# Weight preparation moved to one DMA queue, layer norm fused with the first projection, and the query mean and Wo load moved later

## What is computed

```python
xn = layernorm(x)
q, k, v = (split_heads(xn @ W + b) for W, b in ((Wq,bq),(Wk,bk),(Wv,bv)))
qf, kf, vf = rfft(q), rfft(k), rfft(v)            # over the 2048 positions, 1025 frequencies
idx  = top_k(mean(abs(qf)), 64)                    # per head
attn = softmax(sum(qf.real * kf.real) / 8) at idx
out_freq = mean of qf over the frequencies, everywhere
out_freq[idx] = attn * vf.real[idx]
attn_out = irfft(out_freq) @ Wo + bo
ffn_out  = (silu(xn @ wg) * (xn @ wu)) @ wd        # weights given as int32, scaled by 1/127
result   = x + attn_out + ffn_out
```

## Time and profile before

| | |
|---|---|
| time, median of 2 runs | 6702.76 us (6506.15 and 6899.37) |
| profiled execution | 6235.25 us |
| its span on the slowest core | 6233.7 us (8 cores: 6192.0 to 6233.7) |
| mean granted TensorE clock | 0.868 to 0.870 of full on all cores |
| busy, share of span | TensorE 75%, VectorE 21%, ScalarE 13%, GpSimd 4% |
| moved by DMA | 437.69 MB, 70 GB/s |

### The profile page before, as it was taken

How to read it: one execution, slowest core, us unless ns; L and a number is a source line. 1 busy time by engine, 2 the same in 40 slices (tenths; PEclk the granted TensorE clock), 3 DMA queues, 4 the chain that set the end, 5 groups by cost and what they waited for, 6 DMA issues and landing times.

```text
span 6233.7 us, 52442 instructions; the slowest of 8 cores (6192.0 to 6233.7 us)
## 1 busy us (share of the span) xinstructions
PE 4665.9 (75%) x20720; PEld 1969.4 (32%) x20720; DVE 1306.0 (21%) x1735; ACT 810.5 (13%) x940; POOL 249.8 (4%) x364
## 2 busy tenths in 40 slices
PE   2484627998919884899855884799991888589985
PEld 1131212443403332344322331244440333224442
DVE  3030121011132222111113322101113222211111
ACT  2010101111021111111003111111102111111100
POOL 0101000000100000000000000000010000000001
PEclk9796768999959897999976996899995998789998
DMA  3433332112232112111231311211223212211122
GB/s 104 116 83 113 105 98 76 46 39 65 96 114 48 41 51 78 49 48 38 94 107 58 75 48 47 75 49 39 68 91 117 44 41 58 65 57 50 38 89 93
DMA packets 509272, 437.69 MB, mean 70 GB/s; under 512 B 408524, under 2 KB 408652, under 8 KB 509032
## 3 DMA queue, kind: packets, MB, share of 16 engines
q1 hardware_dynamic: 465384, 279.12, 16.4%
q0 software_dynamic: 33280, 117.46, 6.0%
q10 hardware_dynamic: 10368, 37.75, 2.2%
HBM read 365.07 MB, written 69.21 MB: 70 GB/s over the span
## 4 chain that ended last, share of the span: by engine, by line
PE 62%; DMA 25%; DVE 7%; issue 4%; ACT 2%; DVEq 0%; POOL 0%; ACTq 0%; SPq 0%; POOLq 0%
PE pw L506 15%; PE pw L842 11%; PE pw L851 11%; PE pw L465 10%; PE pw L748 4%; PE pw L795 4%; DMA spE<-attn_scr 3%; DMA spB<-x 2%; DMA spA<-x 2%; DMA spE<-Wo 2%; DMA out<-spC 2%; PE pw L473 2%; PE pw L550 1%; DMA out<-spD 1%; ACT r L409 1%
## 5 line engine op out<-in xcount | busy, mean ns | idle before, releaser
L506 PE MATMUL pw<-r,strm 128*128 128x512 bf16 x4096 | 910.4, 386 | 399.0 <-DMA strm<-dft_cos 399.0
L465 PE MATMUL pw<-strm,r 128*128 128x512 bf16 x3072 | 761.6, 401 | 263.3 <-ACT r L477 101.4
L842 PE MATMUL pw<-r,strm 128*128 128x512 bf16 x3072 | 694.4, 379 | 0.0
L851 PE MATMUL pw<-r,strm 128*128 128x512 bf16 x3072 | 694.4, 379 | 0.0
L506 PEld LDWEIGHTS pw<-r,strm 128*128 128x128 bf16 x4096 | 405.7, 99 | 902.1 <-issue 435.7
L883 PE MATMUL pw<-r 128*128 128x512 bf16 x2048 | 470.0, 389 | 99.6 <-DMA r<-wdT_s 62.6
L861 DVE TENSOR_TENSOR r<-strm,pw 128x1024 bf16<-128x1024 bf16 x192 | 234.6, 1222 | 1382.0 <-PE pw L851 1382.0
L465 PEld LDWEIGHTS pw<-strm,r 128*128 128x128 bf16 x3072 | 291.0, 101 | 720.6 <-issue 434.1
L431 PE MATMUL pw<-identb_t,r 128*128 128x128 bf16 x512 | 64.7, 305 | 549.8 <-DVE r L425 493.3
L851 PEld LDWEIGHTS pw<-r,strm 128*128 128x128 bf16 x3072 | 300.6, 98 | 362.4
L842 PEld LDWEIGHTS pw<-r,strm 128*128 128x128 bf16 x3072 | 300.2, 98 | 363.2 <-issue 1.7
(11 more groups left out here) (142 smaller groups left out, 2631.8 us busy)
## 6 DMA issues: line engine op xcount, KB each, us to landing
strm<-dft_cos SPq DMA_DIRECT2D x96, 512.0 KB
r<-x SPq DMA_DIRECT2D x64, 512.0 KB
strm<-wgT_s SPq DMA_DIRECT2D x96, 256.0 KB
strm<-wuT_s SPq DMA_DIRECT2D x96, 256.0 KB
strm<-dft_sinn POOLq DMA_DIRECT2D x32, 512.0 KB, 5.6
spE<-Wo SPq DMA_DIRECT2D x32, 512.0 KB
r<-crt SPq DMA_DIRECT2D x8, 2048.0 KB
r<-cit SPq DMA_DIRECT2D x8, 2048.0 KB
```

Source lines behind the costliest of these rows:

```text
L465: e.matmul(pw[pwi][:, eta * 512:(eta + 1) * 512], xnT[:, dc, tau * 128:(tau + 1) * 128], wv[:, dc, eta * 512:(eta + 1) * 512], start=(dc = ...
L506: e.matmul(pw[pwi][:, eta * 512:(eta + 1) * 512], slotv[:, tau, :], sig[:, tau, eta * 512:(eta + 1) * 512], start=(tau == 0), stop=(tau == ...
L842: e.matmul(pw[pg][:, tq * 512:(tq + 1) * 512], wgv[:, dc, :], xnT[:, dc, th * 1024 + tq * 512:th * 1024 + (tq + 1) * 512], start=(dc == 0) ...
L851: e.matmul(pw[pu][:, tq * 512:(tq + 1) * 512], wuv[:, dc, :], xnT[:, dc, th * 1024 + tq * 512:th * 1024 + (tq + 1) * 512], start=(dc == 0) ...
```

## The change

- The keys sd and gc go. Each prep_chunk loads on SyncE's queue (q) and casts on VectorE (even) or ScalarE (odd). The prep_some calls are four of 18 chunks, around the second and third projection, in place of six of 12.
- prep_attn(nm), empty before, now turns one attention matrix into bfloat16 in DRAM: eight times a load, a cast and a store. It is called in batch 0 for Wq before prefetch_wbuf, for Wk and Wv between the layer norm and the first projection, and for Wo after it.
- prefetch_wbuf loads those bfloat16 blocks (256 KB each) straight into wbuf, without buffer or cast; prefetch_wo does the same, into all of wbuf, so Wo now takes groups 0 to 7 of strm. prefetch_wo moves behind phase_fft(b, 2).
- For b >= 1 a new phase_ln_proj(b) replaces prefetch_wbuf(b, 0), phase_ln and phase_proj(b, 0).
- The body of phase_qmean moves to the head of phase_middle_b.

```diff
@@ prep_attn, called in batch 0
-        pass
+        for dc in range(8):
+            par = dc % 2
+            sp = ("spA", "spB")[par]
+            bp = ("spC", "spD")[par]
+            em("q", ... e.dma_start(out=xstage[par], in_=W_ins[nm][dc * 128:(dc + 1) * 128, :]),
+               writes=[sp], dma=True)
+            em("v" if par == 0 else "s", ... (bstage[par][:, 0:1024], xstage[par]),
+               reads=[sp], writes=[bp])
+            em("q", ... e.dma_start(out=w_scr[nm][dc * 128:(dc + 1) * 128, :], in_=bstage[par][:, 0:1024]),
+               reads=[bp], writes=[f"scr{nm}"], dma=True)
@@ prep_chunk
-        em("sd", ... e.dma_start(out=it, in_=src_ap), writes=itk, dma=True)
-        em("gc", ... e.tensor_copy(bt, it), reads=itk, writes=btk2)
+        em("q", ... e.dma_start(out=it, in_=src_ap), writes=itk, dma=True)
+        if par == 0:
+            em("v", ... e.tensor_copy(bt, it), reads=itk, writes=btk2)
+        else:
+            em("s", ... e.copy(bt, it), reads=itk, writes=btk2)
         em("q", ... e.dma_start(out=dst_ap, in_=bt), reads=btk2, writes=[dtk], dma=True)
@@ prefetch_wbuf (prefetch_wo likewise, from w_scr["Wo"])
-            em("q", ... e.dma_start(out=xstage[par], in_=W_ins[nm][...]), writes=[sp], dma=True)
-            em("v" if par == 0 else "s", ... (wbuf[:, dc, :], xstage[par]), reads=[sp], writes=gr("st", ...))
+            em("q", ... e.dma_start(out=wbuf[:, dc, :], in_=w_scr[nm][dc * 128:(dc + 1) * 128, :]),
+               reads=[f"scr{nm}"], writes=gr("st", dc * 1024, (dc + 1) * 1024), dma=True)
@@ new: phase_ln_proj(b), its order of emission
+        for tau in range(4):
+            lndma(tau)
+        prefetch_wbuf(b, 0)
+        for tau in range(16):
+            lnchain(tau)          # v: sum, mean, mean^2, variance, 1/s, normalise; s: Square, Sqrt
+            if tau + 4 < 16:
+                lndma(tau + 4)
+            transp(tau)           # t: 8 transposes into pw2/pw3; s: copy to xnT
+            if tau >= 1:
+                projmms(tau - 1)  # t: 16 + 2 matmuls into pw0/pw1; v: copy to sig
+        projmms(15)
@@ the loop over batches
-        prefetch_wbuf(b, 0)
-        phase_ln(b)
         if b == 0:
-            prep_some(12)
-        phase_proj(b, 0)
-        if b == 0:
-            prep_some(12)
+            prep_attn("Wq")
+            prefetch_wbuf(b, 0)
+            phase_ln(b)
+            prep_attn("Wk")
+            prep_attn("Wv")
+            phase_proj(b, 0)
+            prep_attn("Wo")
+        else:
+            phase_ln_proj(b)
         phase_fft(b, 0)
-        phase_qmean(b)
         prefetch_wbuf(b, 1)
         if b == 0:
-            prep_some(12)
+            prep_some(18)
         phase_proj(b, 1)
@@ (the next three prep_some(12) become 18 likewise)
         phase_middle_pre(b)
         phase_middle_a(b)
+        phase_fft(b, 2)
         prefetch_wo(b)
-        phase_fft(b, 2)
         phase_middle_b(b)
```

More of the change, by code:

```diff
@@ L21 @@
 C1 = float(1.0 / (np.sqrt(DH) + 1e-8))
-ENGS = ("t", "v", "s", "q", "g", "sd", "gc")
-STREAM_OF = {"sd": "s", "gc": "g"}
+ENGS = ("t", "v", "s", "q", "g")
 class Sched:
     def __init__(self):
-        self.ops = {e: [] for e in ENGS if e not in STREAM_OF}
+        self.ops = {e: [] for e in ENGS}
         self.cnt = {e: 0 for e in ENGS}
@@ L40, in emit_fence @@
         bnd = self.cnt[e]
-        self.ops[STREAM_OF.get(e, e)].append((None, [(e, bnd)], False, 0, e, "dmafence"))
+        self.ops[e].append((None, [(e, bnd)], False, 0, "dmafence"))
         self.seen[e][e] = bnd
@@ L85, in emit @@
         amt = 16 if dma else 1
-        self.ops[STREAM_OF.get(e, e)].append((fn, sorted(waits.items()), inc, amt, e, tag))
+        self.ops[e].append((fn, sorted(waits.items()), inc, amt, tag))
         self.nops += 1
@@ L444, in prefetch_wbuf @@
         for dc in range(8):
[L445 to L452, removed]
+            em("q", lambda e, nm=nm, dc=dc:
+               e.dma_start(out=wbuf[:, dc, :], in_=w_scr[nm][dc * 128:(dc + 1) * 128, :]),
+               reads=[f"scr{nm}"], writes=gr("st", dc * 1024, (dc + 1) * 1024), dma=True)
     def phase_proj(b, si):
@@ L580, in phase_fft @@
                 em("g", lambda e: e.dma_start(out=dbg["d_qn"], in_=nyq_qr[:]), reads=["nyq_qr"], dma=True)
[L582 to L610, removed]
     def phase_middle_pre(b):
@@ L655, in phase_middle_b @@
     def phase_middle_b(b):
+        for (vsp, reg, nrow, nrtk, dst, dtk, pwi) in [
+                (qr_v, "r3", nyq_qr, "nyq_qr", qmr, "qmr", 0),
+                (qi_v, "r4", None, None, qmi, "qmi", 1)]:
+            for phi in range(8):
+                last = (phi == 7 and nrow is None)
+                for eta in range(2):
+                    em("t", lambda e, vsp=vsp, phi=phi, eta=eta, pwi=pwi, last=last:
+                       e.matmul(pw[pwi][0:1, eta * 512:(eta + 1) * 512], onescol[:],
+                                vsp[:, phi, eta * 512:(eta + 1) * 512],
+                                start=(phi == 0), stop=last),
+                       reads=gr(reg, phi * 1024, (phi + 1) * 1024) + ["onescol"],
+                       writes=[f"pw{pwi}"], inc=(last and eta == 1))
+            if nrow is not None:
+                for eta in range(2):
+                    em("t", lambda e, nrow=nrow, eta=eta, pwi=pwi:
+                       e.matmul(pw[pwi][0:1, eta * 512:(eta + 1) * 512], onesrow[0:1, 0:1],
+                                nrow[0:1, eta * 512:(eta + 1) * 512], start=False, stop=True),
+                       reads=[nrtk, "onesrow"], writes=[f"pw{pwi}"], inc=(eta == 1))
+            em("s", lambda e, dst=dst, pwi=pwi: e.mul(dst[:], pw[pwi][0:1, :], 1.0 / NF),
+               reads=[f"pw{pwi}"], writes=[dtk])
+        for (qrow, qrtk, qt, qttk, pwi) in [(qmr, "qmr", qtr, "qtr", 0), (qmi, "qmi", qti, "qti", 1)]:
+            for eta in range(2):
+                em("t", lambda e, qrow=qrow, eta=eta, pwi=pwi:
+                   e.matmul(pw[pwi][0:16, eta * 512:(eta + 1) * 512], onesrow[0:1, 0:16],
+                            qrow[0:1, eta * 512:(eta + 1) * 512], start=True, stop=True),
+                   reads=[qrtk, "onesrow"], writes=[f"pw{pwi}"], inc=(eta == 1))
+            em("v", lambda e, qt=qt, pwi=pwi: e.tensor_mul(qt[:], pw[pwi][0:16, 0:1024], eexp_t[:]),
+               reads=[f"pw{pwi}", "eexp"], writes=[qttk])
         if debug and b == 0:
@@ L766, in phase_irfft @@
                reads=gr("r6", 0, 8192), dma=True)
[L768 to L776, removed]
     def prefetch_wo(b):
-        wostage = spE[:].bitcast(F32)[:, 0:1024]
         for dc in range(8):
             em("q", lambda e, dc=dc:
[L782 to L786, removed]
+               e.dma_start(out=wbuf[:, dc, :], in_=w_scr["Wo"][dc * 128:(dc + 1) * 128, :]),
+               reads=["scrWo"], writes=gr("st", dc * 1024, (dc + 1) * 1024), dma=True)
     def phase_wo(b):
@@ L953, in run_engine @@
     def run_engine(ekey, eng):
-        for (fn, waits, inc, amt, semkey, tag) in S.ops[ekey]:
+        for (fn, waits, inc, amt, tag) in S.ops[ekey]:
             for (pe, pv) in waits:
@@ L960, in run_engine @@
             if inc and inst is not None:
-                inst.then_inc(SEMS[semkey], amt)
+                inst.then_inc(SEMS[ekey], amt)
     @block.sync
```

89 lines of the change are left out of this document (78 added, 11 removed).

## The result

| | before | after |
|---|---|---|
| median of all runs, us | 6596.37 (11 runs, 6228.67 to 6940.67) | 6420.57 (12 runs, 6289.2 to 6954.99) |
| profiled execution, us | 6235.25 | 6291.62 |
| span of the slowest core, us | 6233.7 | 6290.0 |
| mean granted clock | 0.868 to 0.870 | 0.874 to 0.878 |

The ratio is 1.0095, 95% interval 1.0062 to 1.0128: the changed kernel is 0.95% slower.

The account below looks back on a forecast made before the run. TensorE bounds the kernel, with holes (busy 75% of the span). Batch 0 +292 us and three batches -229 us give +63 us on 6235.25, 6298 us, +1.0%, carried to the median as 6770 us; range 6250 to 6960.

Parts of the forecast that it names:

- first transform: Batch 0: starts at 389 us against 295.0, +94 us including the delays before it, behind the Wo chunks and cosine load.
- (a) fused stage, collision: Head of batches 1 to 3: fused layer norm and projection +11 us; x loads colliding with final additions' loads +5 us.
- turn of the ring: Fused stage: one tile's path through VectorE and TensorE and back, 12.4 us (10.2 to 13.9 by granted clock).
- (b) Wk: Before the second projection, batches 1 to 3: Wk blocks land in time for a dense start, gain 35 us.
- (c) Wv: Before the third projection, batches 1 to 3: Wv loads partly under Nyquist, 4 to 5 us stay, gain 23 us.
- (d) middle: Third projection to transform, batches 1 to 3: transform starts before the Wo loads but waits behind the Exp, gain 50 us.
- (e) mean: Query mean, now ahead of phase_middle_b with nothing beside it, batches 1 to 3: +11 us.
- (f) net's first weights: Net, batches 1 to 3: first weights wait for the last Wo matmul, one load and clock, +4.5 us.
- the dear store (1): Batch 0 chunks: each store takes 3.03 us, chunks 8.0 us, together +177 us, +2.8%, 6880 us; chance 0.15.
- The fused stage at half clock throughout (2): Batches 1 to 3: +1.5 us on 42 turns, together +126 us, +2.0%, 6838 us; chance 0.15.
- The free single queue (3): Batch 0: next load runs beside the store, 4.2 us a chunk, together -131 us, -2.1%, 6560 us; chance 0.07.
- (4): Third transform's early start worth nothing because the Exp blocks all of it: +45 us more, 6820 us; chance 0.08.

Follow-up runs that it names:

- the filler experiment: Changed kernel plus 18 further matmuls with unused results after each tile's own in the fused stage; 6164.56 us, ratio 0.9841.

## Why the prediction was right or wrong

| step | predicted, us | measured, us |
|---|---|---|
| chunk on the single queue | 6.9 | 6.92 |
| first x load | +46 | +45.7 |
| first transform | +94 | +101.7 |
| second transform | +201 | +211.0 |
| Nyquist of the third ends | +277 | +288.1 |
| end of batch 0 | +292 | +303.7 |
| (a) fused stage, collision | +11, +5 | +5.5, +2 |
| turn of the ring | 12.4 | 11.9 |
| (b) Wk | -35 | -36.0 |
| (c) Wv | -23 | -20.1 |
| (d) middle | -50 | -51.9 |
| (e) mean | +11 | +11.2 |
| (f) net's first weights | +4.5 | +5.0 |
| a batch of 1 to 3 | -76.5 | -82.4 |
| sum | +63 | +56 |

The sum and the ratio (1.010 against 1.0095) are right, and nearly all terms with them. That the sum is only 7 us off is partly luck: batch 0 came out 11.7 us longer than forecast and the three others together 18 us shorter. (The measured terms of batch 1 are differences between the two traces: for (c), Nyquist's end to the projection's end at 2588.09, 74.1 us against 94.2; for (d) from there to Nyquist's end, 82.7 against 134.6; for the collision, the last down matmul to the last addition, 46.1 against 44.1. They add up to -84 us; the inverse transform's first half, with its table loads, took 2 us more.)

Three steps failed. The second is the one that makes the forecast, "within 2%" and with it no change, wrong.

First, the level. I carried the ratio to the median of two runs, 6770 us; the median came out at 6420.57. My text had said that nothing in one profile explains the gap between profile and median, and then used that median as a base. The base that the sum was made against gave 6298 us, and the runs that the ratio rests on took 6289 to 6330. Only the width of the range, taken over both levels, held the time.

Second, the step from the sum to the outcome. I wrote that a measurement can tell about 2% from no change, and gave no row for it. Six of the seven runs that the ratio rests on lie within 0.12% (6289.2 to 6296.72, one at 6330.17), and the interval is 0.66% wide. So "within 2%" is what happened, and the move is nevertheless real: slower by 0.95%, beyond its interval, where "no change" had got my largest chance. A sum of +1.0% should have been stated as slower.

Third, a small term of batch 0. The first projection resumes at 285.05, as forecast, but the chunks behind it go on 4 to 5 us later than I took it, and the same holds behind the other two. In both kernels four tiles are done when the wait begins and twelve remain. The end of the second projection, first in the kernel before (TensorE's last tile and ScalarE's issue of the next chunk's load), then in the changed one (the next chunk's cast):

```profile
551.31 3.63 PE L465 MATMUL pw<-strm,r 128*128 128x512 bf16 x16
...
551.54 0.33 ACTq L379 DMA_DIRECT2D spA<-wu  x1
```

```profile
695.83 0.68 DVE L390 CAST spC<-spA 128x1024 bf16<-128x1024 int32 x1
```

Before, the next load stood in ScalarE's list behind the copy of the last even tile, and went out while TensorE was still at the last odd one: 48.1 us from resumption (503.41) to load. After, the next cast stands in VectorE's list behind the copy of that last odd tile: 52.8 us from resumption (643.08) to cast. I had taken the shorter time for both. At the first transform 7.7 us are missing from the forecast, 4 to 5 of them this tile and 3 the first store of Wo, which took 5.06 us (338.90) while GpSimd's queue loaded a sine table (issued at 337.02). The other two projections add some 4 us each, and other small terms give about 4 back, which leaves 11.7 at the end of batch 0.

Of the rivals, the dear store (1) did not occur, all cores storing at once or not: of the 100 stores on the chain 94 took 1.98 to 2.08 us, five up to 2.5 and one the 5.06 above. (Its 6880 us are the sum added, not the ratio carried over as elsewhere, which would give 6893; nothing hangs on it.) The fused stage at half clock throughout (2) did not either: the bursts mostly alternate between 4.85 and 5.98 us, where 3.56 us is the full clock and twice that would be the half one, so the clock comes back within each. The free single queue (3) is ruled out by the period of 6.92 us. (4) was no rival: the transform kept its 50 us.

The Trainium skill (TensorE: Matmul & The Clock Gate, § HAM oscillation) warns that waits between matmul bursts throttle the array again each time. The trace agrees at each of the 42 turns, whose bursts took 4.3 to 6.2 us, and by the filler experiment it cost 2.35 us a turn. The same page (§ Part 4, PE-mode transpose) says that the full clock doesn't engage for transposes, since they don't count as activity in the same way. Here the eight ran in 0.61 us within dense matmuls and in 1.01 us behind the gap, so they do profit from the full clock; whether they help to hold it, no run shows. From both rules together I had put the turn nearer 13.9 us; it was 11.9.

## What to carry to other kernels

- On a queue that waits for each of its transfers, a stage costs the sum of all that stands in its line, the casts of other engines too. Emit the next load ahead of the last store, or give load and store a queue each, before asking what they cost.
- Fusing two stages pays only if no engine's list has the consumer's copy ahead of the next tile's preparation. Follow one tile round the lists; if the path returns to its start, the fused stage takes the sum, and the gaps take the clock as well.
- Make the forecast on the level of the execution that the trace shows, and say separately where a median of few runs may fall.

## What the runs showed of the hardware that I had not expected

- Work added made the kernel faster: 18 unused matmuls in a gap of 5 us took a turn from 11.9 to 9.56 us. The gap cost matmuls (4.85 to 5.98 us in place of 3.45 for 16) and transposes (1.01 in place of 0.61 us for eight).
- In the kernel with the attention matrices cast once, cores 0 and 1 were granted 0.81 in a single stage of batch 0 while cores 2 to 7 had 0.94 to 0.96: 135 us for a transform that takes 113. Their later transforms took what the others' did (58.2 against 57.6 us for the second), and core 1 ended at 6175.6 to 6177.4 us in all three executions.
- A cast of 128x1024 from int32 to bfloat16 took 693 ns on VectorE, as from float32 (690).
